# Four neighbouring nodes in each partition: a new layout for the units of a graph kernel

## What is computed

```python
Ws = 0.5 * (W + swapaxes(W, -1, -2))        # W: (8, 2048, 2048)
A = sigmoid(U @ U.T)                        # U: (2048, 16), one gate for all graphs
K = Ws * A
d = rsqrt(maximum(K.sum(-1), EPS))
y = w_scale * einsum('bnm,bmc->bnc', K * d[:, :, None] * d[:, None, :], x)
out = layernorm(x + y, axis=-1)             # x: (8, 2048, 64)
```

## Time and profile before

| | before |
|---|---|
| median of 3 runs | 464.98 us (462.67 to 467.94) |
| the profiled execution | 463.4 us |
| its span in the profile | 461.6 us |
| granted TensorE clock, mean | 0.99 |
| PE, DVE, ACT, POOL busy | 433.8, 412.7, 207.8, 116.8 us |
| moved by DMA | 143.09 MB, 310 GB/s |

### The profile page before, as it was taken

One profiled execution on the slowest core, in us unless ns is written; L12 is line 12 of the kernel. 1 busy time (PEld: TensorE's weight loads), 2 busy tenths in 40 slices (PEclk: granted clock), 3 DMA queues, 4 the chain that ended last, 5 costly groups with the idle time before them and its releaser, 6 DMA issues.

```text
span 461.6 us, 14416 instructions
## 1 busy us (share of the span) xinstructions
PE 433.8 (94%) x5302; PEld 227.9 (49%) x5302; DVE 412.7 (89%) x1153; ACT 207.8 (45%) x655; POOL 116.8 (25%) x134
## 2 busy tenths in 40 slices
PE   7887999999998999999999999999999999999993
PEld 6555444554444544554445544554445544555341
DVE  6988777999899988999899989999899998999645
ACT  3797332654254433553426442554426543454311
POOL 0000000013340334203340234203340234303444
PEclk9999899999999999999999999999999999999997
DMA  8999699988999799998999999998999999996012
GB/s 284 387 315 389 223 381 355 350 286 313 369 350 304 277 364 355 372 282 324 383 340 354 316 328 342 389 284 322 386 338 357 325 318 343 386 285 232 2 43 49
DMA packets 101386, 143.09 MB, mean 310 GB/s; under 512 B 35824, under 2 KB 35824, under 8 KB 101360
## 3 DMA queue, kind: packets, MB, share of 16 engines
q1 hardware_dynamic: 86496, 139.01, 85.7%
q10 hardware_dynamic: 14864, 3.74, 4.2%
HBM read 138.54 MB, written 4.19 MB: 309 GB/s over the span
## 4 chain that ended last, share of the span: by engine, by line
PE 81%; DVE 7%; ACT 6%; issue 3%; DMA 2%; POOLq 0%; POOL 0%; DVEq 0%; SPq 0%
PE yp L449 46%; PE kt L407 15%; PE tw L407 15%; ACT k L574 3%; DVE k L691 2%; DVE k L680 2%; ACT gate L561 2%; PE yp L550 2%; PE yp L469 2%; DMA k<-in_adj_dram 1%; PE yp L482 1%; DMA h<-in_L_gnn_U_dram 1%; PE kt L493 1%; DVE ut_a L671 0%; DVE var L739 0%
## 5 line engine op out<-in xcount | busy, mean ns | idle before, releaser
L574 ACT ACTIVATE k<-kt 128x512 f32<-128x512 f32 (+3 forms) x288 | 149.3, 523 | 222.6 <-PE kt L407 222.5
L449 PE MATMUL yp<-k,z 128*64 128x512 f32 x960 | 239.0, 611 | 0.0
L680 DVE TENSOR_TENSOR k<-tw,k 128x512 f32<-128x512 f32 (+2 forms) x320 | 193.3, 604 | 22.3 <-PE tw L407 17.9
L691 DVE CUSTOM_DVE_ANT_0 k<-k,gate 128x512 f32<-128x512 f32 (+2 forms) x320 | 196.1, 613 | 0.0
L407 PEld LDWEIGHTS tw<-ident,k 64*128 64x128 f32 x2176 | 80.6, 139 | 79.7 <-issue 74.4
L407 PEld LDWEIGHTS kt<-ident,k 64*128 64x128 f32 x1920 | 73.7, 139 | 62.4 <-issue 48.8
L407 PE MATMUL kt<-ident,k 64*128 64x64 f32 x1920 | 91.6, 228 | 13.0 <-ACT k L574 11.7
L407 PE MATMUL tw<-ident,k 64*128 64x64 f32 x2176 | 98.6, 228 | 2.9 <-issue 1.5
L449 PEld LDWEIGHTS yp<-k,z 128*64 128x64 f32 x960 | 56.5, 136 | 66.6 <-issue 55.3
L329 POOL TENSOR_TENSOR d<-deg,minus_half 128x4 f32<-128x4 f32 x32 | 32.4, 1012 | 197.6 <-DVE deg L701 197.6
L574 ACT ACTIVATION_READ_ACCUMULATOR k<-kt 128x1 f32 x288 | 57.2, 199 | 0.0
(11 more groups left out here) (54 smaller groups left out, 130.2 us busy)
## 6 DMA issues: line engine op xcount, KB each, us to landing
k<-in_adj_dram SPq DMA_DIRECT2D x128, 1024.0 KB, 7.3
xt<-in_x_dram ACTq DMA_DIRECT2D x7, 512.0 KB, 9.0
out_dram<-h SPq DMA_DIRECT2D x7, 512.0 KB, 9.5
xt<-in_x_dram SPq DMA_DIRECT2D x1, 512.0 KB, 14.0
out_dram<-k SPq DMA_DIRECT2D x2, 128.0 KB, 2.1
out_dram<-k SPq DMA_DIRECT2D x3, 64.0 KB, 1.7
h<-in_L_gnn_U_dram SPq DMA_DIRECT2D x1, 128.0 KB, 3.3
out_dram<-k ACTq DMA_DIRECT2D x1, 64.0 KB, 1.9
```

The lines of the kernel that those rows point to most:

```text
L449: t = pe.matmul(yp[at:at + C, m // 2, :], z[:, n * G + c, :], K[(n, m)][:, c, :], start=(q == first_unit[m] and c == 0), stop=(q == last_u ...
L574: nc.scalar.activation(K[(j, i)][:, r, c0:UW].rearrange("p (c h e) -> p c h e", h=2, e=H), whole_rows(kt[:, 0:2, :], r % 2, (UW - c0) // P ...
L680: nc.vector.tensor_tensor(row, whole_rows(tw[:, tw_bank[g] // 2 * 2:tw_bank[g] // 2 * 2 + 2, :], g % 2, w // P), row, ALU.add).then_inc(su ...
L691: nc.vector.tensor_tensor_reduce(row, row, A[:, A_AT[g]:A_AT[g] + w], 1.0, 0.0, ALU.mult, ALU.add, deg_parts[:, i * G + r, j:j + 1]).then_ ...
```

## The change

Partition p of chunk g now holds row 4 p + g of the unit instead of row 128 g + p. A partition therefore holds four neighbouring nodes. Four consequences follow:

- x and the output lie in SBUF with four neighbouring nodes in a row, and their DMAs move 1 KB at a time. The adjacency still comes in rows of 2 KB.
- Columns stay in the order of memory, so the 128 columns that belong to chunk c are c, c + 4, c + 8, ... Each block that PE transposes is taken with a step of four elements (16 bytes).
- The transposed blocks lie in PSUM as before, one after the other. DVE and ACT read them with chunks innermost, that is in steps of 64 elements, and read and write K contiguously.
- `ut_a` keeps the order in which u is transposed; `ut_b` is in node order. The outer products are always 512 wide, and the sigmoid of a diagonal row takes from them the columns that it needs. Rows of diagonal units have runs of 1 to 3 columns out of 4.

```diff
+        def columns_of(row, c):
+            return row.rearrange("p (e c) -> p c e", c=G)[:, c, :]
+        def columns_from_to(row, c0, c1):
+            return row.rearrange("p (e c) -> p e c", c=G)[:, :, c0:c1]
+        def chunk_by_chunk(row, c0, c1):
+            return row.rearrange("p (h e c) -> p h e c", h=2, c=G)[:, :, :, c0:c1]
         def whole_rows(t, slot, chunks):
             return (t[:, :, HALF_ROW * slot:HALF_ROW * slot + H * chunks]
-                    .rearrange("p h (c e) -> p c h e", e=H))
+                    .rearrange("p h (c e) -> p h e c", e=H))
...
         def rows_of(t, b):
-            return t[b, :, :].rearrange("(n p) c -> p n c", p=P)
+            return t[b, :, :].rearrange("(i p g) c -> p i (g c)", p=P, g=G)
+        def by_unit(t):
+            return t[:, :, :].rearrange("p (i g) c -> p i (g c)", g=G)
...
-                src = adj[b, i * UW:(i + 1) * UW, j * UW:(j + 1) * UW].rearrange("(g p) m -> p g m", p=P)
+                src = adj[b, i * UW:(i + 1) * UW, j * UW:(j + 1) * UW].rearrange("(p g) m -> p g m", p=P)
...
-                sp.dma_start(rows_of(out, b), h[:, :, :]).then_inc(h_moved, 16)
+                sp.dma_start(rows_of(out, b), by_unit(h)).then_inc(h_moved, 16)
...
                     transpose_halves(tw_banks(g), HALF_ROW * (g % 2),
-                                     [K[(j, i)][:, c, row * P:(row + 1) * P] for c in range(lower_width(s, row) // P)]
+                                     [columns_of(K[(j, i)][:, c, :], row) for c in range(lower_width(s, row) // P)]
...
-                                     [K[(i, j)][:, c, row * P:(row + 1) * P]
+                                     [columns_of(K[(i, j)][:, c, :], row)
...
-                    t = pe.transpose(yp[:, k, c * P:(c + 1) * P], y_sb[:, k, c * P:(c + 1) * P], ident[:, :])
+                    t = pe.transpose(yp[:, k, c * P:(c + 1) * P], columns_of(y_sb[:, k, :], c), ident[:, :])
...
-                w = lower_width(s, r)
-                pe.matmul(yp[:, g % 2, 0:w], ut_a[:, (i * G + r) * P:(i * G + r + 1) * P],
-                          ut_b[:, j * UW:j * UW + w], start=True, stop=True).then_inc(uu_done, 1)
+                pe.matmul(yp[:, g % 2, :], ut_a[:, (i * G + r) * P:(i * G + r + 1) * P],
+                          ut_b[:, j * UW:(j + 1) * UW], start=True, stop=True).then_inc(uu_done, 1)
...
-                nc.scalar.activation(K[(j, i)][:, r, c0:UW].rearrange("p (c h e) -> p c h e", h=2, e=H),
-                                     whole_rows(kt[:, 0:2, :], r % 2, (UW - c0) // P), ACT.Copy,
+                nc.scalar.activation(chunk_by_chunk(K[(j, i)][:, r, :], c0, G),
+                                     whole_rows(kt[:, 0:2, :], r % 2, G - c0), ACT.Copy,
...
-                nc.vector.tensor_copy(ut_columns(ut_a, k), ut_bank(2 * k)).then_inc(ut_a_copied, 1)
+                nc.vector.tensor_copy(ut_a[:, k * UW:(k + 1) * UW], kt[:, 2 * k % KT_RING, :]).then_inc(ut_a_copied, 1)
...
-                row = K[STEPS[s]][:, r, 0:w].rearrange("p (c h e) -> p c h e", h=2, e=H)
+                row = chunk_by_chunk(K[STEPS[s]][:, r, :], 0, w // P)
```

More of the change, by code:

```diff
@@ L186, in last_store @@
             k, c0, c1 = PIECES[piece]
-            n0 = 8 * k + 4 * half
-            return (rows_of(out, B - 1)[:, n0 + c0:n0 + c1, :],
+            i = 2 * k + half
+            return (out[B - 1, i * UW:(i + 1) * UW, :].rearrange("(p g) c -> p g c", g=G)[:, c0:c1, :],
                     piece_of(K[(1, 0)], piece).rearrange("p (c half e) -> p half c e", half=2, e=C)[:, half, :, :])
@@ L193, in last_sums @@
             k, c0, c1 = PIECES[piece]
-            return yp[:, k, 0:c1 * P] if c0 == 0 else kt[:, 0, 0:(c1 - c0) * P]
+            if c0:
+                return kt[:, 0, 0:(c1 - c0) * P].rearrange("p (e c) -> p e c", c=c1 - c0)
+            return columns_from_to(yp[:, k, :], c0, c1) if c1 < G else yp[:, k, :]
         def piece_rows(piece):
@@ L258, in _ @@
                 if k == X_AFTER:
-                    sp.dma_start(xt[:, :, :], rows_of(x, 0)).then_inc(x_loaded, 16)
+                    sp.dma_start(by_unit(xt), rows_of(x, 0)).then_inc(x_loaded, 16)
                 if n in ((3, 2), (2, 3)):
@@ L458, in transpose_last_y @@
                     pe.wait_ge(sum_done, B * NL)
-                width = piece_of(K[(0, 0)], piece).shape[1]
-                for c in range(width // P):
-                    t = pe.transpose(tw[:, piece, c * P:(c + 1) * P], piece_of(K[(0, 0)], piece)[:, c * P:(c + 1) * P],
+                k, c0, c1 = PIECES[piece]
+                for c in range(c0, c1):
+                    t = pe.transpose(tw[:, piece, (c - c0) * P:(c - c0 + 1) * P], columns_of(K[(0, 0)][:, k, :], c),
                                      ident[:, :])
@@ L539, in _ @@
             for piece, (k, c0, c1) in enumerate(PIECES):
-                columns = slice(c0 * P, c1 * P)
                 chunks = [(pair, c) for pair in LAST_PAIRS[k] for c in range(G)]
@@ L548, in _ @@
                         half = (m % 2) * C
-                        y = last_sums(piece)[half:half + C, :]
-                        t = pe.matmul(y, z[:, n * G + c, :], K[(n, m)][:, c, columns],
+                        y, columns = last_sums(piece)[half:half + C], K[(n, m)][:, c, :]
+                        if c1 - c0 < G:
+                            columns = columns_from_to(columns, c0, c1)
+                        t = pe.matmul(y, z[:, n * G + c, :], columns,
                                       start=(c0 > 0 and at == 0), stop=(at == len(chunks) - 1))
@@ L560, in gate_row @@
                 act.wait_ge(uu_done, g + 1)
-                nc.scalar.activation(A[:, A_AT[g]:A_AT[g] + w], yp[:, g % 2, 0:w],
+                gate, sums = A[:, A_AT[g]:A_AT[g] + w], yp[:, g % 2, :]
+                if w < UW:
+                    gate = gate.rearrange("p (e c) -> p e c", c=w // P)
+                    sums = columns_from_to(sums, 0, w // P)
+                nc.scalar.activation(gate, sums,
                                      ACT.Sigmoid).then_inc(gate_ready, 1)
@@ L570, in upper_row @@
                 g = UPPER.index((s, r))
-                c0, part = (0, i) if i != j else (P * (r + 1), 4)
+                c0, part = (0, i) if i != j else (r + 1, 4)
                 n = j * G + r
                 act.wait_ge(kt_done, b * NU + (g - r % 2 + min(2, upper_rows(s) - r // 2 * 2)))
-                nc.scalar.activation(K[(j, i)][:, r, c0:UW].rearrange("p (c h e) -> p c h e", h=2, e=H),
-                                     whole_rows(kt[:, 0:2, :], r % 2, (UW - c0) // P), ACT.Copy,
+                nc.scalar.activation(chunk_by_chunk(K[(j, i)][:, r, :], c0, G),
+                                     whole_rows(kt[:, 0:2, :], r % 2, G - c0), ACT.Copy,
                                      accum_out=deg_parts[:, n, part:part + 1]).then_inc(upper_done, 1)
@@ L597, in load_x @@
             def load_x(b):
-                act.dma_start(xt[:, :, :], rows_of(x, b)).then_inc(x_loaded, 16)
+                act.dma_start(by_unit(xt), rows_of(x, b)).then_inc(x_loaded, 16)
             def uppers_at(b, row, lag):
@@ L686, in gate_product @@
                 w = lower_width(s, r)
-                row = K[(i, j)][:, r, 0:w]
+                row, gate = K[(i, j)][:, r, :], A[:, A_AT[g]:A_AT[g] + w]
+                if w < UW:
+                    row, gate = columns_from_to(row, 0, w // P), gate.rearrange("p (e c) -> p e c", c=w // P)
                 if first:
@@ L690, in gate_product @@
                 dve.wait_ge(sum_done, b * NL + (g + 1))
-                nc.vector.tensor_tensor_reduce(row, row, A[:, A_AT[g]:A_AT[g] + w], 1.0, 0.0, ALU.mult, ALU.add,
+                nc.vector.tensor_tensor_reduce(row, row, gate, 1.0, 0.0, ALU.mult, ALU.add,
                                                deg_parts[:, i * G + r, j:j + 1]).then_inc(lower_done, 1)
@@ L781, in join_last_y @@
                 dve.wait_ge(y_copied, 2 * B - 2 + piece)
-                y = piece_of(K[(0, 0)], piece)
+                y = columns_from_to(K[(0, 0)][:, PIECES[piece][0], :], *PIECES[piece][1:])
                 nc.vector.tensor_tensor(y, last_sums(piece), y, ALU.add).then_inc(y_copied, 1)
```

## The result

The changed kernel takes 575.65 us in the median, against 464.17 for the one before (4 runs each). The ratio is 1.239, with a 95% interval of 1.233 to 1.245. The forecast was 548 us, and 575 as the range's upper end: the time lies just above that end. The direction and the main cause are as forecast, the size is not. One execution of the four, at 583.62, was in a slower state of the chip and is left out of the ratio. The profiled execution took 576.06 us, 574.3 of it span, so 112.7 us are to be explained.

The account below looks back on a forecast made before the run. PE was taken to bound the kernel (51.21 of 52.35 us a batch), its transposes' weight loads uncovered. 463.4 us plus 85 for slower loads, other terms taken as 0, gave 548 us; range 458 to 575 for 8 in 10.

Parts of the forecast that it names:

- The weight load has no cover: In PE's half transposes, load and stream are about equal, so the load is at its limit in every 63 ns pair.
- half rate: Weight load of the half transposes with a step: 107 ns instead of 53, overlap kept, 117 ns a pair; chance 0.60.
- +102 to +111 us: Slower weight loads on PE, summed over 2048 pairs of half transposes, before anything is hidden.
- Net 102 - 17: The lower end of the transposes' extra time, less what PE's idle time hides: 85 us.
- +85: The net extra time taken for the whole kernel, from a range of 85 to 111 us.
- +50 to +54 ns: Extra time for each pair of half transposes on PE, from weight columns standing 16 bytes apart.
- What hides: PE's idle time takes up extra transpose time: up to 9.0 us in the first batch, 8 in seven later ones.
- a step is free at half the load's rate: Strided copies of u^T by DVE and ACT were read as showing a 16-byte step free at about one element per ns.
- rival B: Weight loads on PE don't mind the step and transfers were hidden anyway: 461 to 465 us; chance 0.21.
- The adjacency moves as before: Adjacency loads keep 2 KB rows, 512 a unit; only which rows a partition gets differs; DMA's sum taken as 0.
- rival D: A PSUM read with a step halves DVE's pace, +18.0 us a batch: 579 us; chance 0.07.
- C: Freed DMA time, 1.3 us per transfer, removes the waits for loads, all of them 6.9 us: 456.5 us; chance 0.12.

Follow-up runs that it names:

- e1: Kernel before, with only the 128 weight columns of each transpose taken four apart: 576.18 us, ratio 1.242.
- e7: Kernel before, with weight columns four apart but only 64 loaded instead of 128: 462.63 us, ratio 0.999.
- e3: Changed kernel, with the weight columns of the transposes two apart instead of four: 578.96 us.
- e5: Kernel before, with each load putting four neighbouring adjacency rows into one partition: 496.24 us, ratio 1.070.
- e6: Changed kernel, with both the step of the weights and the order of rows in a load undone: 464.05 us, ratio 1.003.
- e12: Kernel before, with only x and the output moved in 1 KB pieces (except the last output): 462.19 us, ratio 0.998.

## Where the prediction went wrong: the sum behind 548, not the mechanism

- *What held.* The weight load has no cover: with the step alone (e1) all of the time is there, and with half the columns (e7) none of it. A strided load runs at about half rate and the overlap is kept: 121 ns a pair against 117 forecast.
- *The step that failed* is the sum, "+102 to +111 us", "Net 102 - 17", "+85". The span grew by 112.7 us, so 27.7 more than 85. PE's busy time grew by 123.5 (433.8 to 557.3) and its idle time fell by 10.8 (27.8 to 17.0). Against these stand three terms, sized by busy times whose ends are modelled:
  - *The price of a pair.* Of +50 to +54 ns the lower end was taken, 102 us. The half transposes' busy time grew by 113, about 11 more.
  - *What hides.* 17 us of PE's idle time were to be filled, 10.8 were: 6 more. Most of it is the first batch. In the stretch up to the 20 product matmuls at 69.27 us (now 85.35) 4.0 us were filled, not 9.0: PE's busy time grew by 20.1 (59.3 to 79.4), the stretch by 16.1. In the rest 6.8 were filled, of 8.
  - *Terms at nothing or not there.* About 10 us. The products' busy time grew by 3.5 us (239.0 to 242.5), which goes with the clock: three times more than before it fell to the 1.2 GHz level for a few us beside products, and by the two batches above one fall costs 1.5 us. Transposes of u took 2.6 us more (5.1 to 7.7), since PE was slow for longer at the start: four of them took 1.06 us at 5.88 us and 0.60 at 15.58, where before the second four, at 5.58 us, already took 0.60. The profile grants 1.00 in both stretches, so that this is the clock too is argued from the pace; e3 starts as slowly and e1 does not, so it isn't the step. The transposes of y took 2.3 us more (9.2 to 11.5; forecast 0, at most 3.4), the outer products 1.5 (15.9 to 17.4; at most 1.3), the last products in pieces of two chunks 0.4.
- *The earlier trace rows were misread, and half rate owes something to luck.* `ut_columns` (L231) runs over the columns as 4 p + n, that is in the order of memory: these copies write SBUF without a step and read PSUM 128 elements apart. The rows do show what the prediction said no row shows, a PSUM read with a step, and show it free. They say nothing of a step in SBUF, so "a step is free at half the load's rate", the reason given for half rate, and "16 bytes are free on two other engines", the reason for rival B, had no row behind them. Where the changed kernel does step through SBUF by single columns, DVE and ACT slow down (405 against 288 ns, 415 against 278).
- *The reason for half rate*, that each column stood in 16 bytes of its own, was wrong as well: two apart costs the same (e3). The rule weighed there, from the Trainium skill, "Advanced Engine Details and Errata", section Memory Cachelines, has two hits on a 16-byte line as enough; for fp32 weights the run says they are not, and the measurement decides. The step that the Trainium skill, "SBUF — State Buffer", Door 1, counts as free, four fp32, takes 121 ns a pair here against 63.
- *The adjacency moves as before.* Wrong, and it didn't show in the time, since it costs 33 us alone (e5) and next to nothing once PE is the slower (e1, with the old order, takes as long as the changed kernel). The prediction looked at bytes and sizes of rows and not at which rows follow each other.
- *PSUM reads with a step* (rival D): free, as taken, 5 ns and 1 ns in 600. *Runs of one column* were taken as free by the earlier trace rows and are not: +117 and +113 ns on DVE and +137 on ACT in 128 columns. Hidden here.
- *Rivals B and C*: of "the transfers were hidden anyway" against "the freed time comes out", e6 and e12 say the first.

## What to carry to other kernels

Before a layout puts a step into an operand of TensorE, look whether that side is covered: a weight load that is as long as the stream beside it turns any step into time at once, and in fp32 a step of two costs as much as one of four. The order of the rows in a load can cost 33 us with all sizes the same. Undo one thing at a time, since a cost can lie hidden under a bigger one, as these 33 us did, and be all that is seen once the bigger is mended. Before a row is taken as evidence for a step, work out from the access which side has it. A transfer that nobody waits for is not worth a layout: 1 KB instead of 256 B was to free some 20 us of DMA time and gave 1.4 us, hardly to be told from nothing.

## What the runs showed of the hardware that was not expected

- fp32 operands of TensorE keep their pace as long as columns come in neighbouring pairs: runs of two columns out of four are nearly free for the stream (2.48 us against 2.38), and a step of 2 or 4 between single columns about halves the pace, for weights (121 ns against 63 a pair) and for the stream (3.80 us for eight matmuls against 1.94). DVE and ACT show the same in SBUF: single columns four apart cost about one ns more each (405 against 288 ns and 415 against 278 for 128), runs of two on DVE nothing to speak of (422 against 418 for 256). The strided weight load takes 1.04 us a burst at the 1.2 GHz level and 1.06 at 2.4 GHz.
- The clock can fall while PE has no gap of note. In the changed kernel two windows (the columns are those of the two batches above) read

```profile
255.00:257.00 2.00, 1.87 (x20) 1.68 (x20) 0.37 (x2) 0.66 (x3) 0.00 (x0) 0.88 1.03 387
257.00:259.00 2.00, 2.00 (x8) 0.59 (x8) 1.91 (x5) 0.60 (x3) 0.45 (x1) 0.50 1.05 401
```

and the timeline of PE around them

```profile
251.82 0.75 PE L485 MATMUL yp<-ident,y_sb 128*128 128x128 f32 x4
252.50 1.17 PE L423 MATMUL kt<-ident,k 64*128 64x64 f32 x16
253.51 1.12 PE L423 MATMUL tw<-ident,k 64*128 64x64 f32 x16
255.13 1.17 PE L423 MATMUL kt<-ident,k 64*128 64x64 f32 x16 [0.49 <-ACT k L594]
256.23 1.02 PE L485 MATMUL yp<-ident,y_sb 128*128 128x128 f32 x4
257.18 3.28 PE L465 MATMUL yp<-k,z 128*64 128x512 f32 x8
```

From 251.8 us on PE had done nothing but transposes for over 5 us, with one gap of 0.49 us; then the clock was at 0.50 and eight product matmuls took 3.28 us. The kernel before shows such a fall once, in its first batch; this one shows three more, each two batches after the last. The stretch is longer with bursts of 1.06 us instead of 0.58, but it isn't enough: the batch before this one has the same order of work, and its eight product matmuls at 190.91 us took 1.94 us. What brings the clock down is open.
- Two loads of the same bytes, in rows of the same 2 KB, differ by 1.8 us in landing (9.1 against 7.3) through the order of rows alone.
